# Experts' weighted rows added by index into four sums in DRAM, in place of six gathered rows per token

## The chip, the core and the metric

The kernel runs on one core of a Trainium2 chip. The metric is the device time of one execution in microseconds (us). All numbers of the profile are from one execution, taken by the hardware profiler. Engines are PE (TensorE), DVE (VectorE), ACT (ScalarE), POOL (GpSimd) and SP (SyncE, which only issues transfers here).

## What is computed

Four sequences of 512 tokens of 256 numbers, 2048 tokens in all, go through six residual blocks:

```python
x = x + 0.5 * _L0_ffn_ref(_layernorm(x), ...)   # 64 experts, the best 6 per token, and a shared one
x = x + _L0_attn_ref(_layernorm(x), ...)        # gated linear attention, 8 heads
x = x + 0.5 * _L0_ffn_ref(_layernorm(x), ...)   # the same experts again
x = x + 0.5 * _L1_ffn_ref(_layernorm(x), ...)   # 8 experts, all computed, gated
x = x + _L1_attn_ref(_layernorm(x), ...)        # softmax attention over a latent, 16 heads
x = x + 0.5 * _L1_ffn_ref(_layernorm(x), ...)
```

The change concerns the first and third line, which we call the expert layer:

```python
scores = softmax(x @ gate_weight.T)              # 64 experts in 8 groups, 3 groups kept
topk_w, topk_i = top_k(masked scores, 6)
pos = place of this token among those of its expert, in order of tokens
slot = expert * 96 + min(pos, 95)                # 96 slots per expert
buf = zeros(64 * 96, 256).at[slot].set(x[tok])   # so slot 95 keeps the last token sent there
out = (silu(buf @ Wg.T) * (buf @ Wu.T)) @ Wd.T   # per expert, 96 rows
y = sum over k of out[slot[k]] * topk_w[k]       # six rows per token
return y + shared(x)
```

There are 12288 choices for 6144 slots, so most experts overflow. All tokens past place 94 of an expert share its slot 95, and each adds the output of that one slot by its own weight.

## The kernel before

The stream x stays in SBUF as 16 tiles of 128 tokens (`k.X`). Each engine has its own instruction list in the order in which the code emits it, and waits on semaphores; nothing is reordered at run time. The program is a row of blocks, and at the end of each all engines meet.

**Routing** (`route`, once per expert layer, tile pairs m = 0 to 7). ACT normalises, SP stores the normalised rows to `xn_rows` in DRAM, PE computes the logits, DVE finds the best six experts, PE counts the places with triangular matrices, and DVE and POOL make one-hot rows from which PE builds `k.table` (96 slots by 64 experts, the token in each slot). For each token and choice DVE also writes the weight (L987) and the slot number (L904, L908). The shared expert runs in between: `gate_up`, `down` in two halves per quarter of the tokens (L697), and DVE's addition to x (L914). SP also loads the weights of the first 12 experts. The last half of `down` and its addition stand behind the table.

**Experts** (`routed_experts`, steps s = 0 to 66). In step s PE transposes the gathered rows of expert s (L1148), multiplies those of expert s-1 by gate and up (L1157), transposes the hidden rows of expert s-2 and multiplies those of s-3 by the down weights (L1174). ACT evicts the result to `sb_e_y` (L1201) and stores it to `slot_rows` in DRAM (L1203); there are two such buffers. POOL gathers 96 rows of 1 KB for each expert (L1131) into four buffers, each free again once PE has transposed it. SP loads 544 KB of weights for expert e when expert e-12 is done with its buffers.

**Combination**. In the next block POOL gathers, for each tile of 128 tokens, six sets of 128 rows from `slot_rows` (L1236), and DVE adds each by its weight to x (L1250). For the first expert layer this is in `linear_attention`, for the second in `dense_experts`. There POOL runs up to two tiles ahead, and DVE's six additions per tile are spread between the operations of a tile three places earlier. In `linear_attention` the tiles 0 to 3 come ahead of everything else; while POOL gathers them, PE folds weights of the later attention together (`fold`, L1512 and L1518) in the two score banks.

Of the kernel before, what the change touches and what calls it, by code (L numbers as in the profile page):

```python
# [5 lines left out]
ALU = mybir.AluOpType  # L6
# [20 lines left out]
AHEAD = 12  # L27
MS = 352
# [40 lines left out]
class Kit:  # L69


    def __init__(self, nc, ctx):
        self.nc, self.ctx, self.sems = nc, ctx, {}
# [4 lines left out]
    def sem(self, name):  # L78
        if name not in self.sems:
            self.sems[name] = self.ctx.enter_context(self.nc.semaphore(name))  # L80
        return self.sems[name]

# [24 lines left out]
def load_and_prepare(nc, k, w):  # L107
# [3 lines left out]
    with ExitStack() as ctx:  # L111
# [3 lines left out]
        def _(sp):  # L115
            for q in range(NT // 4):
                sp.dma_start(k.X[:, 4 * q:4 * q + 4, :], w["x"].rearrange("(q n p) d -> q p n d", p=P, n=4)[q])\
                  .then_inc(k.sem(f"x_loaded{q}"), 16)
# [7 lines left out]
        def _(pool):  # L126
# [9 lines left out]
            s.mark(pool.memset(k.chunk_keep[:, :], 1.0))  # L136
# [13 lines left out]

            s.mark(pool.memset(k.chunk_keep[:, :].rearrange("p (c s) -> p c s", s=SUB)[:, :, 0:1], 0.0))
# [40 lines left out]
def dense_experts(nc, k, r, store=None, combine=None):  # L192
# [17 lines left out]
    with ExitStack() as ctx:  # L210
# [22 lines left out]
        if combine is not None:  # L233
            rows = [[sb(f"c{combine}_rows{u}_{j}", [P, D]) for j in range(TOPK)] for u in range(2)]
# [4 lines left out]
        ps_e = [ps(f"d{r}_ps_e{j}", [P, 2, D]) for j in range(NP)]  # L239
        block = ctx.enter_context(nc.Block())  # L240
# [14 lines left out]
        def _(pe):  # L255
# [47 lines left out]

            transposed(0, 0)
            logits(0, 0)
            pe.wait_ge(we_low, (r + 1) * DC)
            tiles(pe, tile)

        @block.scalar
        def _(act):  # L310
# [33 lines left out]
            act.preload_act_table_set("natural_log_exp_and_others")  # L344
            act.wait_ge(k.sem("we1_loaded"), 16 * DC)
# [9 lines left out]
        if combine is not None:  # L355
            @block.gpsimd
            def _(pool):
                for n in range(NT):
                    gather_tile(pool, k, combine, n, n % 2, rows)

        @block.vector
        def _(dve):
# [9 lines left out]
            def statistics(n, u):  # L372
# [3 lines left out]
                if combine is not None:  # L376
                    rows_all_added(dve, k, combine, n)
# [7 lines left out]
            def add(n, u, *which):  # L385

                if combine is not None and live(n):
                    for j in which:
                        add_row(dve, k, combine, n, u, rows, j)
# [71 lines left out]
            def tile(n, u):  # L461
# [5 lines left out]
                add(n + 3, 1 - u, 0)  # L467
# [4 lines left out]
                add(n + 3, 1 - u, 1)  # L472
                weigh_odd(n, u, 1)
                add(n + 3, 1 - u, 2)
# [3 lines left out]
                add(n + 3, 1 - u, 3)  # L478

                def last_even():  # L480
                    weigh_even(n, u, 3)
                    add(n + 3, 1 - u, 4)

                def add_up():
# [3 lines left out]
                    add(n + 3, 1 - u, 5)  # L488
# [12 lines left out]

            for n in range(2):
                add(n, n, *range(TOPK))
# [8 lines left out]
            add(2, 0, *range(TOPK))  # L512
# [13 lines left out]
def route(nc, k, r):  # L526
# [7 lines left out]
    XB = 4  # L534
# [1955 lines left out]
```

## Time and profile before

| | us |
|---|---|
| median of 3 runs (lowest, highest) | 1840.82 (1838.76, 1846.98) |
| the profiled execution | 1830.69 |
| its span, first to last instruction | 1829.0 |
| PE, DVE, ACT, POOL busy | 1545.8, 1081.9, 766.6, 684.5 |
| mean granted TensorE clock | 0.932 of full |

The stages by the profile: routing 0 to 132 us, experts 132 to 303, linear attention 303 to 682, routing 682 to 804, experts 804 to 971, dense experts 971 to 1181, latent attention 1181 to 1695, dense experts 1695 to 1829. A share of busy time is a mean over stages that have different limits, so the stages are read one by one.

### The profile page before, as it was taken

The page shows a single profiled execution, that of the slowest core. Times are in us where ns is not written, and L with a number is a line of the kernel's source. Part 1 is how long each engine was busy: PE and PEld are TensorE (multiplying, and loading weights), DVE is VectorE, ACT ScalarE, POOL GpSimd, SP SyncE. Part 2 cuts the span into 40 slices and gives each one's busy share as a digit, 9 for nine tenths or more (in the row PEclk, how much of TensorE's full clock was granted, in tenths as well). Part 3 has the DMA queues.
Part 4 walks back from the last instruction along what each step waited for, and adds up shares of the span by engine and source line. Part 5 has one row for each costly group of instructions (what it writes and reads, how often), then busy time and mean ns, then how long its engine had stood idle before and what let it go on. Part 6 is the DMA issues. An engine that isn't in the chain of part 4 may idle for free. (4 is left out here: it accounts for less than half of the span.)

```text
span 1829.0 us, 26202 instructions
## 1 busy us (share of the span) xinstructions
PE 1545.8 (85%) x7678; PEld 1015.6 (56%) x7678; DVE 1081.9 (59%) x2737; ACT 766.6 (42%) x1822; POOL 684.5 (37%) x675
## 2 busy tenths in 40 slices
PE   6869995658888978869993778699999999998798
PEld 3546663425555544546662656455666666665576
DVE  6842222576775547822224888477766766663788
ACT  5523332356455435533332111266655556553211
POOL 3543333753200004633335553065545555553000
PEclk9989998679999988989996898799999999999899
DMA  8309995321100015129972221000000000000000
GB/s 245 91 12 255 296 298 177 106 65 48 35 1 1 1 44 149 48 84 285 299 230 84 77 77 52 1 0 1 1 1 1 1 1 1 1 1 1 9 17 21
DMA packets 83395, 142.55 MB, mean 78 GB/s; under 512 B 15816, under 2 KB 43312, under 8 KB 83296
## 3 DMA queue, kind: packets, MB, share of 16 engines
q1 hardware_dynamic: 53600, 90.96, 17.0%
q0 software_dynamic: 15360, 37.77, 6.9%
q10 hardware_dynamic: 14336, 12.59, 2.4%
q8 instruction: 52, 0.85, 0.2%
q14 instruction: 47, 0.39, 0.1%
HBM read 122.39 MB, written 18.87 MB: 77 GB/s over the span
## 5 line engine op out<-in xcount | busy, mean ns | idle before, releaser
L2239 POOL TENSOR_TENSOR sb_m_prob<-sb_m_prob,sb_m_rinv 128x512 f32<-128x512 f32 x256 | 258.6, 1040 | 286.1 <-DVE sb_m_rinv L2288 286.1
L2195 ACT ACTIVATE sb_m_prob<-m_ps_s,sb_m_nmax 128x512 f32<-128x512 f32 x256 | 173.6, 683 | 205.4 <-DVE sb_m_nmax L2292 205.4
L2292 DVE TENSOR_REDUCE sb_m_nmax<-m_ps_s 128x2 f32<-128x1024 f32 x128 | 156.3, 1222 | 128.0 <-PE m_ps_s L2090 127.9
L1236 POOL DMA_INDIRECT sb_c_rows<-slot_rows,sb_slot x192 | 191.4, 997 | 107.1 <-issue 51.6
L1131 POOL DMA_INDIRECT sb_e_x<-xn_rows,sb_table x128 | 117.7, 919 | 223.9 <-PE e_ps_x L1148 184.1
L1219 DVE TENSOR_TENSOR sb_e_h<-sb_e_sg,e_ps_gu 96x176 f32<-96x176 f32 x128 | 42.7, 333 | 259.7 <-ACT sb_e_sg L1195 259.7
L1157 PE MATMUL e_ps_gu<-e_wgu,sb_e_xT 128*96 128x352 f32 x512 | 180.1, 475 | 12.1 <-ACT sb_e_xT L1189 11.4
L2098 PE MATMUL m_ps_p<-sb_ident,sb_m_prob 128*128 128x128 f32 x1024 | 136.8, 274 | 15.8 <-ACT sb_m_pT L2203 11.3
L2098 PEld LDWEIGHTS m_ps_p<-sb_ident,sb_m_prob 128*128 128x128 f32 x1024 | 118.4, 141 | 41.2 <-POOL sb_m_prob L2239 14.4
L1174 PE MATMUL e_ps_y<-e_wdn,sb_e_hT 96*96 96x256 f32 x512 | 131.4, 380 | 0.0
L2089 PE MATMUL m_ps_s<-sb_m_latT_high,sb_m_qa 128*128 128x512 f32 x256 | 126.0, 492 | 1.8 <-ACT sb_m_prob L2195 1.8
L2109 PE MATMUL m_ps_v<-sb_m_pT,sb_m_lat 128*64 128x512 f32 x512 | 123.7, 605 | 0.9 <-DVE sb_m_oT L2303 0.9
L1250 DVE SCALAR_TENSOR_TENSOR sb_x<-sb_c_rows,sb_weight,sb_x 128x256 f32<-128x256 f32 (+1 forms) x192 | 92.8, 483 | 41.8 <-DMA sb_c_rows<-slot_rows,sb_slot 38.5
L686 PE MATMUL s_ps<-sb_r_xnT,sb_sguT 128*128 128x512 f32 (+1 forms) x192 | 101.1, 676 | 6.5 <-ACT sb_s_up L782 6.5
L281 PE MATMUL d_ps_e<-sb_d_we_high,sb_d_xT_high 128*128 128x512 f32 x256 | 98.6, 468 | 7.5 <-DVE sb_d_xT_low L402 7.5
L1157 PEld LDWEIGHTS e_ps_gu<-e_wgu,sb_e_xT 128*96 128x96 f32 x512 | 75.5, 167 | 52.6 <-issue 10.0
L2090 PE MATMUL m_ps_s<-sb_m_latT_low,sb_m_qa 128*128 128x512 f32 x256 | 102.1, 399 | 0.0
L1201 ACT ACTIVATE sb_e_y<-e_ps_y 96x256 f32<-96x256 f32 x128 | 48.6, 379 | 118.4 <-DMA slot_rows<-sb_e_y 90.2
L1189 ACT ACTIVATE sb_e_xT<-e_ps_x 128x192 f32<-128x192 f32 x128 | 42.3, 330 | 117.2 <-PE e_ps_x L1148 46.1
L2299 DVE COPY sb_m_pT<-m_ps_p 128x512 f32<-128x512 f32 x128 | 86.5, 676 | 3.8 <-PE m_ps_p L2098 3.8
L1746 POOL TENSOR_TENSOR sb_g_gw<-sb_g_g,sb_g_sig 128x512 f32<-128x512 f32 x8 | 10.9, 1363 | 206.0 <-ACT sb_g_sig L1658 206.0
L1434 PE MATMUL g_bank<-sb_g_xT,sb_wq 128*128 128x512 f32 x128 | 66.7, 649 | 24.9 <-ACT sb_g_zm L1619 24.8
(274 smaller groups left out, 3231.3 us busy)
## 6 DMA issues: line engine op xcount, KB each, us to landing
e_wgu<-wgu SPq DMA_DIRECT2D x128, 352.0 KB, 4.8
e_wdn<-wdn SPq DMA_DIRECT2D x128, 192.0 KB, 4.5
slot_rows<-sb_e_y ACTq DMA_DIRECT2D x128, 96.0 KB, 4.3
xn_rows<-sb_r_xn SPq DMA_DIRECT2D x16, 256.0 KB, 2.2
sb_c_rows<-slot_rows,sb_slot POOLq DMA_INDIRECT x192, 2.8
sb_x<-x SPq DMA_DIRECT2D x4, 512.0 KB, 5.3
sb_e_x<-xn_rows,sb_table POOLq DMA_INDIRECT x128, 5.0
sb_g_zm<-wqT SPq DMA_DIRECT2D x1, 2048.0 KB, 8.9
```

The source lines that it names most:

```text
L686: ins = pe.matmul(ps_s[which][0:rows, :], k.sguT[:, d, which * MS + m0:which * MS + m0 + rows], xnT[:, d, q * QT:(q + 1) * QT], start=(d = ...
L1131: pool.indirect_dma_start(x[u][:, :], None, k.xn_rows[:, :], bass.IndirectOffsetOnAxis(ap=k.table[:, e:e + 1], axis=0)).then_inc(got[u], 16)
L1157: ins = pe.matmul(ps_gu[v][:, :], xT[v][:, c, :], wgu[(u - 1) % U][:, c, :], start=(c == 0), stop=(c == DC - 1))
L1174: ins = pe.matmul(ps_y[v][:, :], hT[v][:, c, :], wdn[(u - 3) % U][:, c, :], start=(c == 0), stop=(c == 1))
L1236: pool.indirect_dma_start(rows[u][j][:, :], None, k.slot_rows[:, :], bass.IndirectOffsetOnAxis(ap=k.slot[:, n, j:j + 1], axis=0))\
L2089: pe.matmul(to[:, hh, :], q[:, hh, cols], latT[b % 2][0][:, :], start=True, stop=False)
L2090: ins = pe.matmul(to[:, hh, :], q[:, hh, cols], latT[b % 2][1][:, :], start=False, stop=True)
L2098: ins = pe.transpose(ps_p[hh][:, t, :], prob[s % 4][:, hh, t * P:(t + 1) * P], k.ident[:, :])
L2109: ins = pe.matmul(ps_v[rows_of(hh), :], lat[pair // PAIRS % 2][:, t, :], pT[pair % 2][hh][:, t, :], start=(t == 0), stop=(t == TB - 1))
L2195: act.activation(prob[s % 4][:, hh, :], ps_s[s % 2][:, hh, :], ACT.Exp, bias=nmax[s % 2][:, hh:hh + 1], accum_out=rsum[s % 2][:, hh:hh + 1 ...
L2239: pool.tensor_tensor(part, part, rinv[s % 2][:, hh:hh + 1].to_broadcast([P, T]), ALU.mult)\
L2292: dve.tensor_reduce(nmax[s % 2][:, :], ps_s[s % 2][:, :, :], AX, ALU.max, negate=True).then_inc(nmax_ready, 1)
```

## The change

1. **Routing.** Instead of six weights and slot numbers per token, DVE makes a dense row of 64 weights, splits it by place (`late`: place 95 or later) into `share`, which SP stores behind the normalised row in `xn_rows` (now rows of 320 numbers), and `over`, which stays in SBUF. The table's empty slots get the number of a row past the last token. ACT's queue writes zeros over four sums in DRAM. The last quarter's `down` is moved behind the table, and POOL issues the first four gathers inside the routing block.
2. **Experts.** ACT's eviction scales each row by its weight, which came with the gathered row. POOL adds rows 0 to 94 by index into one of four sums in DRAM (an indirect transfer that accumulates; expert e uses sum e modulo 4), and ACT's queue stores row 95 to `last_out` in SBUF. A gather for expert e+6 is issued behind the addition of expert e, into one of six buffers. There are four `sb_e_y` buffers.
3. **Combination.** SP loads the four sums in order, 128 rows each per tile. DVE adds the four up with one reduction whose input is read at a step of 256 numbers, and adds the total to x. What the shared last slots give is computed ahead of it by PE (`LastSlots`: four groups of four transposes and four products, ACT's copies, DVE's additions).
4. **Linear attention.** Four banks instead of three for projections and one instead of two for scores; the folds move to the slot u = -2.

The core of the diff:

```diff
@@ route, sync
+            def store_share(m):
+                sp.wait_ge(share_ready, g0 + m + 1)
+                sp.dma_start(shares[m], share[m % 2][:, :, :]).then_inc(share_stored[m % 2], 16)
@@ route, tensor
-                    if q:
+                    if q and q < NQ:
                         down(q - 1, 0)
+            counted()
             tabled(NPR - 1)
...
+            pe.wait_ge(unfilled_ready, r + 1)
+            pe.matmul(kept_table, k.ident[0:CAP, 0:CAP], unfilled[:, :], start=False, stop=False)
...
+            pe.wait_ge(gu_copied, 3 * (q0 + NQ))
+            down(NQ - 1, 0)
             down(NQ - 1, 1)
@@ route, scalar
             exps(0)
+            for a in range(SUMS):
+                act.dma_start(k.sums[a][0:N, :].rearrange("(p j) d -> p (j d)", j=NT).rearrange("p (q f) -> p q f", f=512),
+                              k.zeros[:, :].unsqueeze(1).to_broadcast([P, NT * D // 512, 512])).then_inc(zeroed, 16)
...
@@ route, gpsimd
+            last_hidden()
...
+            pool.wait_ge(table_ready, r + 1)
+            for e in range(XB):
+                gather_expert(pool, k, e, k.gathered[e], e)
@@ route, vector
-            def slots_capped(m):
...
-            def slots(m, capped):
...
+            def weights_of(m):
+                for i in range(2):
+                    done = s.mark(dve.scalar_tensor_tensor(out=dense[m % 2][:, i, :], in0=masked[:, i, :],
+                                                           scalar=rsum[:, i:i + 1], in1=member[m % 2][:, i, :],
+                                                           op0=ALU.mult, op1=ALU.mult))
...
+                return s.mark(dve.tensor_scalar(late[:, :, :], ps_p[:, :, :], float(CAP - 1), None, ALU.is_ge))
...
+                dve.scalar_tensor_tensor(out=share[m % 2][:, :, :], in0=dense[m % 2][:, :, :], scalar=0.5, in1=late[:, :, :],
+                                         op0=ALU.mult, op1=ALU.max).then_inc(share_ready, 1)
+                return s.mark(dve.scalar_tensor_tensor(out=k.over[:, pair_of(m), :], in0=dense[m % 2][:, :, :], scalar=0.5,
+                                                       in1=late[:, :, :], op0=ALU.mult, op1=ALU.mult))
@@ routed_experts
-    U, GA, LAG = AHEAD, 4, 3
+    U, GA, LAG = AHEAD, 6, 3
...
-                    pool.wait_ge(xT_raw, g - (GA - 1))
...
+            for e in range(XB, GA):
+                gather_expert(pool, k, e, x[e], e)
+            for e in range(E0):
+                b, earlier = e % SUMS, e // SUMS + r * (E0 // SUMS)
+                pool.wait_ge(y_ready, e + 1 + r * E0)
+                if earlier:
+                    pool.wait_ge(y_added[b], 16 * earlier)
                 pool.sem_inc(k.sem("passed"), 1)
+                pool.indirect_dma_start(k.sums[b][:, :], bass.IndirectOffsetOnAxis(ap=k.table[0:CAP - 1, e:e + 1], axis=0),
+                                        y[b][0:CAP - 1, :], None, compute_op=ALU.add).then_inc(y_added[b], 16)
+                if e + GA < E0:
+                    gather_expert(pool, k, e + GA, x[e % GA], e % GA)
...
-                        act.wait_ge(y_stored[v], (g - (3 + v)) * 8)
-                    act.activation(y[v][:, :], ps_y[v][:, :], ACT.Copy).then_inc(y_ready, 1)
+                    if earlier:
+                        act.wait_ge(y_added[b], 16 * earlier)
+                        act.wait_ge(y_last[b], 16 * earlier)
+                    act.activation(y[b][:, :], ps_y[v][:, :], ACT.Copy, scale=x[e % GA][:, D + e:D + e + 1]).then_inc(y_ready, 1)
                     act.wait_ge(y_ready, g - 2)
-                    act.dma_start(k.slot_rows.rearrange("(e c) d -> e c d", c=CAP)[s - 3], y[v][:, :])\
-                       .then_inc(y_stored[v], 16)
+                    act.dma_start(k.last_out[e:e + 1, :], y[b][CAP - 1:CAP, :]).then_inc(y_last[b], 16)
@@ combination
+def load_sums(sp, k, n, rows, a):
+    for i in range(SUMS):
+        sp.dma_start(rows[a][:, i, :], k.sums[i][n * P:(n + 1) * P, :]).then_inc(k.sem(f"rows_loaded{a}"), 16)
...
+    dve.tensor_reduce(total[:, :], rows[a][:, :, :].rearrange("p i d -> p d i"), AX, ALU.add).then_inc(k.sem("c_rows_summed"), 1)
...
+    dve.tensor_tensor(x, total[:, :], x, ALU.add).then_inc(k.sem("c_rows_added"), 1)
...
+class LastSlots:
+    def all_products(self, pe):
+        self.turn(pe, 0)
+        self.turn(pe, 1)
+        for q in range(NT // 4):
+            self.multiply(pe, q)
+            if q + 2 < NT // 4:
+                self.turn(pe, q + 2)
@@ linear_attention
-    A = 3
+    A = 4
...
-        ps_at = [ps(f"g_ps_at{u}", [P, HG, SUB]) for u in range(2)]
+        ps_at = ps("g_ps_at", [P, HG, SUB])
...
+                if u == -2:
+                    pe.wait_ge(raw_loaded, 48)
+                    pe.wait_ge(shared.out_used, 2 * (NT // 4))
+                    for n in range(FOLDS):
+                        fold(n)
```

POOL's list in the experts block, before (`e_x` are the gathered rows; the two branches are the end of one block and the start of the next):

```order
L853 TENSOR_TENSOR sb_s_gate<-sb_s_gate,sb_s_up 128x1024
L548 UNCONDITIONAL_BRANCH
L1120 UNCONDITIONAL_BRANCH
L1131 DMA sb_e_x<-xn_rows,sb_table 96x256 x64
```

and now, with what each waits for (four of the six buffers are called `e_xn`, `sums` are the sums in DRAM):

```order
L1351 DMA e_xn<-xn_rows,sb_table 96x320 x3
L584 UNCONDITIONAL_BRANCH
L1237 UNCONDITIONAL_BRANCH [waits barrier_Pool_Activation_PE_DVE_SP_gather]
L1351 DMA sb_e_x<-xn_rows,sb_table 96x320 x2
L1247 DMA sums<-sb_e_y,sb_table 2176x256 [waits e_y_ready]
L1351 DMA e_xn<-xn_rows,sb_table 96x320
L1247 DMA sums<-sb_e_y,sb_table 2176x256 [waits e_y_ready]
```

The gathers were a list of their own that waited for PE's transposes; each now stands behind an addition that waits for ACT's eviction.

PE's list at the end of routing, before (`s_ps_d` is the shared expert's `down`, `r_ps_t` the table):

```order
L675 MATMUL r_ps_t<-sb_r_hot_tok,sb_r_hot_pos 96x64 x12
L697 MATMUL s_ps_d<-sb_sdT,sb_s_gate 128x256 x6
L675 MATMUL r_ps_t<-sb_r_hot_tok,sb_r_hot_pos 96x64 x12
L729 MATMUL r_ps_x<-sb_ident,sb_r_last 64x128
L731 MATMUL r_ps_t<-sb_ident,sb_last_slot 96x64
L697 MATMUL s_ps_d<-sb_sdT,sb_s_gate 128x256 x6
```

and now:

```order
L735 MATMUL r_ps_t<-sb_r_hot_tok,sb_r_hot_pos 96x64 x12
L743 MATMUL r_ps_r<-sb_r_member_sum,sb_ones_bf 128x64
L744 MATMUL r_ps_r<-sb_r_member,sb_ones_bf 128x64
L745 MATMUL r_ps_r<-sb_r_member,sb_ones_bf 128x64
L735 MATMUL r_ps_t<-sb_r_hot_tok,sb_r_hot_pos 96x64 x12
L799 MATMUL r_ps_x<-sb_ident,sb_r_last 64x128
L801 MATMUL r_ps_t<-sb_r_unfilled,sb_ident 96x64
L803 MATMUL r_ps_t<-sb_ident,sb_last_slot 96x64
L766 MATMUL s_ps_d<-sb_sdT,sb_s_gate 128x256 x6
L766 MATMUL s_ps<-sb_sdT,sb_s_gate 128x256 x6
```

Both last halves of `down` stand behind the table, and the second has a bank of its own.

## Rows read from the trace of the kernel before

**Rows 1.** Busy PE, PEld, DVE, ACT, POOL, 200 to 240; then clock, DMA share, GB/s.

```profile
200.00:240.00 40.00, 39.13 (x193) 25.68 (x192) 9.34 (x32) 14.57 (x48) 14.70 (x16) 1.00 1.04 301
```

**Rows 2.** Transposes of gathered rows in both experts blocks: last numbers, first and last start.

```profile
L1148 PE MATMUL e_ps_x<-sb_ident,sb_e_x x128: 244/246/423, 131.9 to 293.6; 96*128 96x96 f32 x128
...
L1148 PE MATMUL e_ps_x<-sb_ident,sb_e_x x128: 244/246/423, 804.1 to 961.2; 96*128 96x96 f32 x128
```

**Rows 3.** Who waited for whom in 132 to 303: us, times, longest.

```profile
POOL sb_e_x L1131 <- PE e_ps_x L1148: 94.5, 57, 5.4
ACT sb_e_y L1201 <- DMA slot_rows<-sb_e_y: 50.1, 45, 3.3
```

**Rows 4.** Timeline (start, length) of late steps of the second experts block.

```profile
958.56 0.36 PEld L1148 LDWEIGHTS e_ps_x<-sb_ident,sb_e_x 96*128 96x128 f32 x2
...
960.94 0.36 PEld L1148 LDWEIGHTS e_ps_x<-sb_ident,sb_e_x 96*128 96x128 f32 x2
...
963.74 0.38 ACT L1201 ACTIVATE sb_e_y<-e_ps_y 96x256 f32<-96x256 f32 x1 [0.72 <-PE e_ps_y L1174]
```

**Rows 5.** Median us to landing in 128:136, 200:240, 270:290; last, a queue's total.

```profile
sb_e_x<-xn_rows,sb_table POOLq DMA_INDIRECT x6, 2.6
...
sb_e_x<-xn_rows,sb_table POOLq DMA_INDIRECT x16, 5.1
...
slot_rows<-sb_e_y ACTq DMA_DIRECT2D x9, 96.0 KB, 1.7
...
q0 software_dynamic: 15360, 37.77, 6.9%
```

**Rows 6.** Timeline at the end of the first routing block.

```profile
110.97 2.42 DVE L921 TENSOR_TENSOR sb_s_gate<-sb_s_gate,sb_s_up 96x512 f32<-96x512 f32 x1 [0.30 <-ACT sb_s_gate L788]
...
117.24 4.45 PE L697 MATMUL s_ps_d<-sb_sdT,sb_s_gate 128*128 128x256 f32 x12 [7.02 <-DVE sb_x L914]
...
123.30 0.22 DVE L1044 CAST sb_table<-r_ps_t 96x64 uint32<-96x64 f32 x1 [0.47 <-PE r_ps_t L731]
...
127.07 0.69 DVE L914 SCALAR_TENSOR_TENSOR sb_x<-s_ps_d,sb_x 128x512 f32<-128x512 f32 x1 [2.96 <-PE s_ps_d L697]
...
131.72 0.92 POOL L1131 DMA_INDIRECT sb_e_x<-xn_rows,sb_table  x1 [0.30 <-issue]
```

**Rows 7.** Groups of DVE instructions: three of routing, one of the block at 971.

```profile
L1005 DVE TENSOR_REDUCE sb_r_member<-sb_r_hot 128x128 bf16<-128x768 f32 x8 | 11.8, 1479 | 0.3
...
L900 DVE TENSOR_REDUCE sb_r_posf<-sb_r_picked 128x12 f32<-128x768 f32 x8 | 7.5, 933 | 0.0
...
L976 DVE TENSOR_TENSOR sb_r_masked<-sb_r_ex,r_ps_own 128x128 f32<-128x128 f32 x8 | 2.2, 277 | 0.1
...
L1250 DVE SCALAR_TENSOR_TENSOR sb_x<-sb_c_rows,sb_weight,sb_x 128x256 f32 (+1 forms) x96 | 46.0, 479 | 14.4 <-DMA sb_c_rows<-slot_rows,sb_slot 13.8
```

**Rows 8.** SP's issues (start, length) in routing and in linear attention.

```profile
25.75 0.47 SPq L610 DMA_DIRECT2D e_wgu<-wgu  x1
...
305.54 6.15 SPq L1339 DMA_DIRECT2D sb_g_qp<-wo  x1
```

**Rows 9.** Timeline at the head of linear attention; the last row is its first slot.

```profile
321.40 13.88 PE L1512 MATMUL g_ps_at<-sb_g_kp,sb_g_zm 128*128 128x64 f32 x64 [21.13 <-DMA sb_g_qp<-wo]
...
335.22 5.51 PE L1518 MATMUL g_ps_at<-sb_g_qp,sb_g_kp 128*64 128x256 f32 x32
...
341.61 0.30 ACT L1597 ACTIVATE sb_g_ln_var<-sb_g_mv,sb_eps 128x4 f32<-128x4 f32 x1 [0.24 <-DVE sb_g_mv L1781]
...
378.48 3.78 PE L1434 MATMUL g_bank<-sb_g_xT,sb_wq 128*128 128x512 f32 x4 [22.29 <-ACT sb_g_zm L1619]
```

**Rows 10.** Four transposes at 9 us, and the expert products of both dense blocks.

```profile
9.47 1.11 PE L637 MATMUL r_ps_x<-sb_ident,sb_r_xn 128*128 128x128 f32 x4 [2.77 <-ACT sb_r_xn L756]
...
L281 PEld LDWEIGHTS d_ps_e<-sb_d_we_high,sb_d_xT_high x128: 186/190/338, 998.4 to 1153.2; 128*128 128x128 f32 x128
...
L281 PEld LDWEIGHTS d_ps_e<-sb_d_we_high,sb_d_xT_high x128: 187/190/337, 1706.2 to 1823.2; 128*128 128x128 f32 x128
```

More of the change, by code:

```diff
@@ L239, in dense_experts @@
         ps_e = [ps(f"d{r}_ps_e{j}", [P, 2, D]) for j in range(NP)]
+        if combine is not None:
+            flat = [bank.rearrange("p a d -> p (a d)") for bank in ps_e]
+            shared = LastSlots(k, combine, flat[0:2], flat[2:4], wT)
         block = ctx.enter_context(nc.Block())
@@ L302, in tile @@
                 pair(n, u, 3)
+            if combine is not None:
+                shared.all_products(pe)
             transposed(0, 0)
@@ L306, in _ @@
             pe.wait_ge(we_low, (r + 1) * DC)
+            if combine is not None:
+                pe.wait_ge(shared.out_used, 2 * (combine + 1) * (NT // 4))
             tiles(pe, tile)
@@ L500, in tile @@
                 dve.tensor_tensor(x, ps_b[:, :], x, ALU.add).then_inc(out_ready, 1)
+            if combine is not None:
+                shared.all_added(dve)
             for n in range(2):
-                add(n, n, *range(TOPK))
+                sum_rows(n, n)
+                add_rows(n)
                 statistics(n, n)
@@ L551, in route @@
         nmr = sb(f"r{r}_nmr", [P, NT])
-        xn = [sb(f"r{r}_xn{u}", [P, 2, D]) for u in range(XB)]
+        xn = k.xn
         xnT = sb(f"r{r}_xnT", [P, DC, N])
@@ L562, in route @@
         masked = sb(f"r{r}_masked", [P, 2, E0])
+        rsum = sb(f"r{r}_rsum", [P, 2])
+        dense = [sb(f"r{r}_dense{u}", [P, 2, E0]) for u in range(2)]
+        late = sb(f"r{r}_late", [P, 2, E0])
+        share = [sb(f"r{r}_share{u}", [P, 2, E0]) for u in range(2)]
+        unfilled = sb(f"r{r}_unfilled", [CAP, E0])
         top = sb(f"r{r}_top", [P, 2, 8])
@@ L1309, in linear_attention @@
         gw = [sb(f"g_gw{u}", [P, T]) for u in range(2)]
-        rows = [[sb(f"c0_rows{u}_{j}", [P, D]) for j in range(TOPK)] for u in range(2)]
+        rows = [sb(f"c0_rows{a}", [P, SUMS, D]) for a in range(ROWS)]
+        total = sb("c0_total", [P, D])
         raw = sb("g_raw", [P, 2, 6])
@@ L1577, in _ @@
             pe.wait_ge(w_high, 2)
-            pe.wait_ge(raw_loaded, 48)
-            for n in range(FOLDS):
-                fold(n)
+            shared.all_products(pe)
             transposes(0)
@@ L1707, in slot @@
                     lns(u + 2)
+                if u == -2:
+                    for n in range(FOLDS):
+                        fold_copy(n)
                 if qs:
@@ L1729, in _ @@
             act.activation(k.wo0[:, :, :], k.wo0[:, :, :], ACT.Copy, scale=k.gnorm[:, 0:1]).then_inc(w_high, 1)
-            for n in range(FOLDS):
-                fold_copy(n)
+            shared.all_copies(act)
             deviations(0)
```

343 lines of the change are left out of this document (220 added, 123 removed).

## Prediction, written before the changed kernel ran

> **What bounds the kernel now.** I read the busy time by stretches first, then the first and last start of a few groups, then who waited for whom, and the timeline where a stage turns. In an experts block PE is busy nearly all the time and the DMA engines are saturated [rows 1]: 39.1 of 40 us, at 301 GB/s. The transposes of the gathered rows start once per expert, so their first and last start give the pace [rows 2]: 161.7 us for 63 intervals (2.57 each) and 157.1 (2.49). POOL, which gathers, is far ahead: it waits 94.5 us for PE to free a buffer. ACT waits 50.1 us, 45 times, for a store to land, because there are only two buffers [rows 3]; PE stays busy meanwhile, so those waits are near the limit and not far over it. Late in the block, where no weights are loaded any more (the last 12 steps), a step takes 960.94 - 958.56 = 2.38 us [rows 4]: PE's own pace. In the dense block at 971 it is not PE that sets the pace: its weight loads span 154.8 us there, and only 117.0 in the other dense block, which has the same products and no combination [rows 10]. (154.8 - 117.0)/13 = 2.91 us per tile is six additions of 0.479 us [rows 7] = 2.87.
>
> **Experts.** The change removes the fixed distance between gather and use. The gather for expert e+6 stands behind the addition of expert e, and that waits for ACT's eviction of e, which falls in step e+3. So a ring closes every three steps:
> - from the start of step e+3 to the eviction's end: 963.74 + 0.38 - 960.94 = 3.18 us [rows 4];
> - POOL issues the addition, then the gather: the pitch of one issue is 0.92 + 0.30 = 1.22 [rows 6];
> - from the gather's issue to its landing, L, until step e+6 may start: 2.6 with the queues free, 5.1 saturated [rows 5].
>
> 3P = 3.18 + 1.22 + L, where P is the pace. L = 2.6 gives 2.33, under PE's own 2.38; L = 5.1 gives 3.17. A step now moves 544 KB of weights, 96 rows of 1.25 KB in, and 95 KB out once, or twice if an accumulation reads what it adds to: 759 to 854 KB. At P = 2.93 this is 259 to 291 GB/s, somewhat under the 301 at which L is 5.1. So I take L = 4.4, nearer the loaded row, and P = 2.93. Fifty-one intervals with weight loads and 12 without: 51 x 2.93 + 12 x 2.38 = 178.0, against 161.7 and 157.1: +16.3 and +20.9. At the end an accumulation has to land where a store did, 2.6 against 1.7 [rows 5]: +1 per layer. Sum **+39**. The four output buffers remove the 50.1 us of ACT's waits, but the ring comes in their place. The additions themselves cost POOL an issue each, covered by the 94.5 us it waited.
>
> How 95 accumulated rows cost the queues, no row shows. Lower bound: as the gather's rows, 36864 rows of 1 KB in 6.9% of 16 engines' span of 1829 us [rows 5], 0.055 us per row on its engine, 0.33 for six rows. Upper: on few engines and read and written, rival C.
>
> **Routing.** The last hidden product, 2.42 us of DVE ahead of the table, goes to POOL, and a half of `down`, 4.45, is put behind it: the table, at 123.30, comes about 6.5 earlier. Both halves of `down` then follow each other, 8.9 us, and the last addition (127.07 + 0.69) comes 2.9 earlier [rows 6]. The first gathers are issued at the table and land under `down`, so the 2.5 us between barrier and first transpose that were their landing [rows 2, 5] are gone: -5.4 per layer, **-11**. POOL's issue beside the hidden product hides behind the same 8.9 us; without that cover it would be 3.7 late. DVE per pair: five new instructions, three of 128x128 at 0.28 [rows 7] and two half as wide (0.14 to 0.28), minus three of 12 numbers (0.14, half of it, my choice): +0.7 to 1.0, taken 0.7; DVE waits for PE about half the time here, so half of 16 x 0.7 stays: +6. Thirteen zero writes on ACT's queue at 0.47 each = +6; upper bound, if each of the eight large ones blocks as the load of `wo` did, 6.15 [rows 8], 49. I take 0.47, as most issues have it. Routing together **+1** (-11 + 6 + 6).
>
> **Linear attention.** The shared slots come first, from about 306 (the block's first load stands at 305.54 [rows 8]): four groups, each four transposes of 1.11 [rows 10] and four products of 512 columns, two thirds of the 4.45 us that twelve of 256 took [rows 6] = 2.97 at the low clock; 16.4, and 0.7 for the last addition. Then four tiles, each a reduction, an addition (0.48) and about 0.9 of statistics and gaps. The reduction reads its input at a step, as L1005 does: 1.479/768 per number gives 1.97 us for 1024; as L900, which reads in order, 1.24 [rows 7]. I take 1.97. Tiles ready at 306 + 17.1 + 4 x 3.35 = 336.5, before 341.6 [rows 9]: -5. SP's sums are 512 KB per tile and come under the shared slots. The folds, 13.88 + 5.51 = 19.4 us, fit in the 22.29 us for which PE waited at 378.48 [rows 9]: +1 for the handover; uncovered they would cost 19.4. The fourth bank loosens evictions a little: -4, a guess between 0 and -10. Together **-8**.
>
> **Dense block at 971.** If DVE sets the pace, a tile falls from 2.87 to 1.97 + 0.48 = 2.45: 13 x 0.42 = -6 (with the reduction at 1.24, -15). Its head: 971 + 17.1 + two tiles 6.7 + normalise 0.8 + halves 4.5 + 0.6 = 1000.7, where the first product stood at 998.4 [rows 10]: +2. **-4**.
>
> **Sum.** 39 + 1 - 8 - 4 = +28. The profiled execution took 1830.69, 10 below the median of the three runs, which I take as spread of the runs and not of the work: 1859 on the profile's basis, 1869 on the median's. I say **1870**.
>
> **Rivals.**
> A: as above, L near 4.4.
> B, the other side: the DMA engines have gaps once POOL no longer gathers ahead, and the ring stays near PE's pace. With the other terms at -11, the break-even is 102P + 57.2 + 2 - 318.8 = 11, so P = 2.66 and L = 3.6: below that the kernel is faster. At L = 2.8, P = 2.4, the experts give -15 and the sum is -26: 1815. With the reduction at 1.24 it is -35: 1805. For it: demand at 2.6 us per step is 292 to 328 GB/s only in the loaded 51 steps, and what can't be served at once may fall on the weights, which have 12 steps of room, rather than on the gathers. Against it: in every loaded stretch of before the gathers took 5.1.
> C: 95 rows are spread over fewer DMA engines than 96, since 95 = 5 x 19. Nineteen rows on one engine are 19 x 0.055 = 1.04 us, double or triple if read, added and written, and the gather stands behind them in the same queue: L = 5.1 + 1.5 = 6.6, P = 3.67. 51 x 3.67 + 28.6 = 215.8, twice, less 318.8, +2, -11: +104, 1945. No row of before has 95 rows in a transfer, so the trace bears it neither out nor rules it out.
> (The Trainium skill, "DMA: Bandwidth & Descriptors", section "Why a DMA increments its semaphore by 16 and not by 1", says that a transfer uses the largest number of engines up to 16 that divides the slowest dimensions, which is 5 for 95, with an exception for some direct copies from POOL's queue. By that rule C holds; the 96 rows of before would use 16. It would make the chance of C larger than I give; I hold it down since its price, not its being, needs a saturated queue.)
> D: the zero writes block ACT: of the 49 above, the 6 are in the sum and DVE's work hides part of the rest; +25 over A, 1895.
> E: the gains and the ring cancel, within 0.5%, which is about what a measurement of this kernel can tell from no change.
> That the kernel doesn't do what it says: the zeros, the additions and the reads of the sums are ordered by waits throughout, so I give it nothing.
>
> **Chances.** A 0.42, B 0.29, C 0.16, D 0.05, E 0.08. Faster by over 0.5% is B and a little of A's lower edge (0.02): 0.31; within 0.5%: 0.08; slower: 0.61. A's own range is 1850 to 1895 (L from 3.9 to 5.1). The range for 8 in 10 reaches from B's 1805 to C's 1945.
>
> **What would show it.** The pace of the transposes in the experts blocks, near 2.9 in the loaded part and 2.4 in the last 12, with PE waiting for gathered rows and POOL for `sb_e_y` (A); L by the landing of gathers in the loaded stretch, and of the additions in the same queue; if only a third of the DMA engines work on an addition, C. ACT without waits for stores. ACT's zero issues at 0.47 or longer (D). The table near 117 and the last `down` behind it; first transposes near 126.5. The reduction at 1.97 or 1.24; the head of linear attention at 336; the folds inside the gap before the first projection; the dense block's weight loads over 149 us. The prediction is wrong if the pace stays under 2.66 (faster) or goes above 3.2.

## The result: 14% slower, and the profile after

The changed kernel takes 2092.0 us (median of 4 runs, 2082.2 to 2096.0) against 1839.8 for the kernel before beside it: a ratio of 1.137, 95% interval 1.133 to 1.141. The forecast was 1870, the range 1805 to 1945. The profiled execution spans 2089.4 us where that of before spans 1829.0, so 260.4 us have to be found. Four marks cut the span into stages: the first and last transpose of gathered rows in each experts block, the first statistics of linear attention's head, and the first and last expert product of the dense blocks. The first fence is of the changed kernel, groups of PE, PEld and ACT instructions (after the duration in ns: first and last start); the transposes of one block stand in two groups, by buffer.

```profile
L1263 PE MATMUL e_ps_x<-sb_ident,e_xn x88: 244/305/423, 154.4 to 430.8; 96*128 96x96 f32 x88
...
L1263 PE MATMUL e_ps_x<-sb_ident,e_xn x88: 245/302/424, 946.1 to 1222.7; 96*128 96x96 f32 x88
...
L1782 ACT ACTIVATE sb_g_ln_var<-sb_g_mv,sb_eps x4: 281/292/298, 483.4 to 655.0; 128x4 f32<-128x4 f32 x4
...
L301 PEld LDWEIGHTS d_ps_e<-sb_d_we_high,sb_d_xT_high x128: 186/190/338, 1272.5 to 1413.7; 128*128 128x128 f32 x128
```

With the same marks before [rows 2, 9, 10]:

| stage | before | after | difference |
|---|---|---|---|
| start to first transpose | 131.9 | 154.4 | +22.5 |
| 63 steps of experts, first layer | 161.7 | 276.4 | +114.7 |
| last transpose to head of linear attention ready | 48.0 | 52.6 | +4.6 |
| from there to the first transpose of the second layer | 462.5 | 462.7 | +0.2 |
| 63 steps of experts, second layer | 157.1 | 276.6 | +119.5 |
| last transpose to first dense product | 37.2 | 49.8 | +12.6 |
| dense products with the combination | 154.8 | 141.2 | -13.6 |
| the rest | 675.8 | 675.7 | -0.1 |

Nine tenths of the loss are the two experts blocks, one tenth the routing (the row from the head of linear attention to the second layer is +0.2 only because 5 gained in that block hide 5 lost in the second routing). Who waits there, in 154 to 434 (columns as in [rows 3]), first of POOL's list and then of PE's:

```profile
POOL sums L1247 <- ACT sb_e_y L1318: 79.8, 19, 6.4
POOL sums L1247 <- issue: 12.7, 41, 0.4
...
PE e_ps_x L1263 <- DMA e_xn<-xn_rows,sb_table: 85.6, 22, 5.8
PE e_ps_x L1263 <- DMA sb_e_x<-xn_rows,sb_table: 1.6, 2, 1.0
```

Before, POOL waited for PE and PE for nothing much; now PE waits for gathered rows and POOL for evicted rows, about once in every three experts. Taken over a whole stretch the DMA engines have time left: this is the stretch of [rows 1] again, with PE at 30.3 busy in place of 39.1, the clock at 0.74, a DMA share of 0.61 and 150 GB/s in place of 301.

```profile
200.00:240.00 40.00, 30.25 (x108) 18.33 (x108) 5.41 (x18) 9.67 (x27) 21.76 (x17) 0.74 0.61 150
```

One whole round of the ring, by the timelines of PE (transposes), ACT (evictions) and POOL (start, length, what stood before):

```profile
229.43 0.58 PE L1263 MATMUL e_ps_x<-sb_ident,e_xn 96*128 96x96 f32 x2 [4.18 <-DMA e_xn<-xn_rows,sb_table]
...
234.17 0.43 PE L1263 MATMUL e_ps_x<-sb_ident,e_xn 96*128 96x96 f32 x2
...
234.42 0.47 ACT L1318 ACTIVATE sb_e_y<-e_ps_y,e_xn 96x256 f32<-96x256 f32 x1 [1.72 <-PE e_ps_y L1289]
...
235.87 1.85 POOL L1247 DMA_INDIRECT sums<-sb_e_y,sb_table  x1 [4.35 <-ACT sb_e_y L1318]
...
236.66 0.33 PE L1263 MATMUL e_ps_x<-sb_ident,e_xn 96*128 96x96 f32 x2
...
238.02 0.95 POOL L1351 DMA_INDIRECT e_xn<-xn_rows,sb_table  x1 [0.30 <-issue]
...
239.27 1.85 POOL L1247 DMA_INDIRECT sums<-sb_e_y,sb_table  x1 [0.30 <-issue]
...
243.98 0.58 PE L1263 MATMUL e_ps_x<-sb_ident,e_xn 96*128 96x96 f32 x2 [4.77 <-DMA e_xn<-xn_rows,sb_table]
```

From one late transpose to the next, 14.55 us for three experts: 5.46 to the end of the eviction (234.89), 0.98 until POOL issues the addition, 2.15 until it issues the gather, 5.96 until those rows can be transposed (the view of DMA issues has 5.4 as the median to landing in 200 to 240, 6.5 for additions). This is one of the longer rounds. Over all rounds of the first layer whose first expert stands where this one does (its number divides by three), the trace gives 13.85 on average: 4.97, 0.99, 2.15 and 5.74. The pace of the transposes is 4.52 over the first 51 intervals and 3.83 over the last 12, in the second layer 4.47 and 4.05. So the last 12 do not run at the 2.38 of [rows 4], although no weights are loaded there any more: gathers stand behind additions up to the last gather, that of expert 63.

PE runs three steps in a burst and then stands for 4 us. The three parts of this round, first step, rest of the burst, pause (busy PE, PEld, DVE, ACT, POOL; then clock, DMA share, GB/s):

```profile
229.40:234.20 4.80, 4.77 (x13) 2.85 (x14) 0.60 (x2) 0.64 (x2) 1.82 (x2) 0.50 0.52 102
234.20:239.20 5.00, 5.00 (x25) 3.11 (x23) 1.20 (x4) 2.07 (x6) 2.79 (x2) 0.98 0.57 140
239.20:243.90 4.70, 0.01 (x1) 0.00 (x0) 0.00 (x0) 0.47 (x1) 4.02 (x3) 0.71 0.95 258
```

After the pause the granted clock is 0.50, the lower level, for the whole first step (a pair of transposes takes 0.58, later in the burst 0.33), and that step needs 5.46 to its eviction. A later one takes 3.17, from 234.17 to the eviction's end at 237.34, as [rows 4] had 3.18. The third row shows what the mean of 150 GB/s hides: while PE waits for the gathered rows, the DMA engines are at 0.95 and 258 GB/s.

The routing shows the second loss on ACT's queue (the last group stands in the second layer):

```profile
14.51 16.98 ACTq L873 DMA_DIRECT2D sums<-sb_zeros  x3
31.52 7.66 ACTq L877 DMA_DIRECT2D sums<-sb_zeros  x4
39.21 0.85 ACTq L878 DMA_DIRECT2D xn_rows<-sb_zeros  x1
40.10 0.60 ACT L812 ACTIVATE sb_r_xnT<-r_ps_x 128x512 f32<-128x512 f32 x1 [25.58 <-issue]
...
821.20 10.43 ACTq L873 DMA_DIRECT2D sums<-sb_zeros  x3
```

ACT stood for 25.58 us in the first layer and 10.42 in the second while it issued the zero writes.

### The profile page after: what moved, and what is told of

Same layout as the page of the kernel before. It is cut to its first block and busy times, and to the rows that moved or that the text cites. A ratio compares the mean times of both kernels' runs of the same rounds, so it can differ in the third digit from the quotient of the medians.

```text
span 2089.4 us, 26181 instructions
## 1 busy us (share of the span) xinstructions
PE 1643.9 (79%) x7784; PEld 1063.9 (51%) x7784; DVE 1101.3 (53%) x2657; ACT 781.5 (37%) x1826; POOL 739.3 (35%) x613
## 3 DMA queue, kind: packets, MB, share of 16 engines
q0 software_dynamic: 47104, 28.41, 7.9%
## 5 line engine op out<-in xcount | busy, mean ns | idle before, releaser
L1247 POOL DMA_INDIRECT sums<-sb_e_y,sb_table x128 | 236.5, 1848 | 190.1 <-ACT sb_e_y L1318 163.2
L1272 PE MATMUL e_ps_gu<-e_wgu,sb_e_xT 128*96 128x352 f32 x512 | 221.0, 564 | 0.5 <-ACT sb_e_xT L1304 0.5
L1263 PE MATMUL e_ps_x<-sb_ident,e_xn 96*128 96x96 f32 x176 | 39.1, 316 | 176.3 <-DMA e_xn<-xn_rows,sb_table 173.4
L1289 PE MATMUL e_ps_y<-e_wdn,sb_e_hT 96*96 96x256 f32 x512 | 147.8, 417 | 0.0
L1263 PEld LDWEIGHTS e_ps_x<-sb_ident,e_xn 96*128 96x128 f32 x176 | 25.2, 172 | 203.3 <-DMA e_xn<-xn_rows,sb_table 148.7
L1272 PEld LDWEIGHTS e_ps_gu<-e_wgu,sb_e_xT 128*96 128x96 f32 x512 | 91.1, 201 | 49.3 <-issue 24.8
L1351 POOL DMA_INDIRECT e_xn<-xn_rows,sb_table x88 | 83.5, 949 | 37.3 <-issue 29.7
L1289 PEld LDWEIGHTS e_ps_y<-e_wdn,sb_e_hT 96*96 96x96 f32 x512 | 83.8, 186 | 17.7
```

What stands on the lines that cost most here:

```text
L1247: pool.indirect_dma_start(k.sums[b][:, :], bass.IndirectOffsetOnAxis(ap=k.table[0:CAP - 1, e:e + 1], axis=0), y[b][0:CAP - 1, :], None, co ...
L1272: ins = pe.matmul(ps_gu[v][:, :], xT[v][:, c, :], wgu[(u - 1) % U][:, c, :], start=(c == 0), stop=(c == DC - 1))
L1289: ins = pe.matmul(ps_y[v][:, :], hT[v][:, c, :], wdn[(u - 3) % U][:, c, :], start=(c == 0), stop=(c == 1))
```

## Experiments

Theory (ring): in the experts blocks the round through eviction, addition, gather and landing decides, so more distance between gather and use ends it, down to what POOL can issue. Rivals: the 95 rows of an addition (rival C of the prediction), the adding itself, or the transfers as such. The kernel before took 1874 in the group of e1, e2, e3 and e5, 1864 in that of c_again, e7, e8 and e9, 1840 in that of e10, e11 and e13, and 1839 beside e14, so each ratio is to the kernel before beside it. Blocks are compared by their 63 intervals from first to last transpose; across groups such a comparison carries that difference with it.

### e1_far: twelve buffers

```diff
-    U, GA, LAG = AHEAD, 6, 3
+    U, GA, LAG = AHEAD, 12, 3
```

> Twelve gather buffers instead of six, so the gather of expert e+12 stands behind the addition of e; nothing else. In the changed kernel a round of three experts takes 14.5 us: 1.0 from the eviction to the addition's issue, 2.15 for that issue, 5.96 until the gather has landed, 5.46 until the next eviction. Theory ring: with nine steps of distance in place of three that round is worth 14.5/9 = 1.6 per expert and no longer decides; what is left is POOL's own pitch, 1.85 + 0.30 + 0.95 + 0.30 = 3.40 per expert. 63 x 3.40 = 214 against 276, in both blocks: about 125 less, 1965. Rival queues (the transfers themselves are the limit, whatever the order): the pace stays at 4.4, 2090.

Measured: 1948.9, ratio 1.042 (1.033 to 1.051). The blocks: 201.7 and 202.1 in place of 276. POOL now issues without a stop (timeline of POOL):

```profile
228.82 1.85 POOL L1247 DMA_INDIRECT sums<-sb_e_y,sb_table  x1 [0.30 <-issue]
230.98 0.95 POOL L1351 DMA_INDIRECT sb_e_x<-xn_rows,sb_table  x1 [0.31 <-issue]
232.23 1.85 POOL L1247 DMA_INDIRECT sums<-sb_e_y,sb_table  x1 [0.30 <-issue]
```

The pitch is 232.23 - 228.82 = 3.41. From its first addition to its last POOL issues 52 additions with a gather behind them and 11 without: 52 x 3.41 + 11 x 2.15 = 201.0, and the trace has 203.0 and 200.6. (The expectation had 63 steps at 3.40, with a gather behind each.) A gather is now issued some 15 us ahead of its use in place of 6. The ring was the limit, and POOL's issues are the next one. Transfers as such are refuted: the same bytes were moved 75 us faster per block.

### e2_rows96, e3_plain, e13_rows90: what an addition costs

```diff
@@ e2_rows96
-  IndirectOffsetOnAxis(ap=k.table[0:CAP - 1, e:e + 1], axis=0), y[b][0:CAP - 1, :], None, compute_op=ALU.add)
+  IndirectOffsetOnAxis(ap=k.table[:, e:e + 1], axis=0), y[b][:, :], None, compute_op=ALU.add)
@@ e3_plain
-  y[b][0:CAP - 1, :], None, compute_op=ALU.add)
+  y[b][0:CAP - 1, :], None)
@@ e13_rows90
+  IndirectOffsetOnAxis(ap=k.table[0:90, e:e + 1], axis=0), y[b][0:90, :], None, compute_op=ALU.add)
```

> The addition takes 96 rows in place of 95 (row 95 is then added to its token's sum too, one contribution too many). Rival C, few engines because 95 = 5 x 19: the addition's issue falls from 1.85 towards the gather's 0.95 and its landing from 6.3 to 3 or less, the gather behind it lands at 3 to 4; round (1.0 + 1.25 + 3.5 + 4.0)/3 = 3.2 per expert, 63 x 3.2 = 202 against 276: 1940. Rival accumulation (what costs is that it reads and adds): issue and landing stay, 2090.

> The 95 rows are written by index without adding (the sums are then the last expert's rows). Rival accumulation: issue falls to 0.95 and landing to about 3, 1940. Rival C (95 rows on few engines): issue and landing stay near 1.85 and 6, time near 2090, at most 60 less for the read that is gone.

> The changed kernel with the additions cut to 90 rows (the last five of each expert are not added). Issue of the addition: 95 rows took 1.85 us and 320 packets, 96 rows 1.44 us and 102. If what counts is that 16 divides the number, 90 = 15 x 6 should look like 95: 1.8 us and over 250 packets. If it is only the number of engines that divide it (5 for 95, 15 for 90), 90 looks like 96: 1.4 us, about 100 packets, experts blocks about 237 us and not 276.

What these kernels compute is not the result: with 96 rows the last one is added once too often, plain writes keep only the last expert's rows, and with 90 five rows of each expert are left out.

Measured: 96 rows 2020.5, ratio 1.080 (1.069 to 1.091), blocks 236.7 and 240.0; plain writes of 95 rows 2019.3, 1.079 (1.069 to 1.090), blocks 237.0 and 251.0; 90 rows 2013.5 in one run, blocks 241.6 and 232.1. The first two came out between the values that their expectations set against each other (1940 and 2090). The lines of each page that tell them apart (of the core: all packets, and those under 512 bytes; of the queue: packets, MB, share; of the group: busy, mean ns, then idle time), in the order changed kernel, 96 rows, plain 95, 90 rows:

```profile
DMA packets 136729, 156.09 MB, mean 75 GB/s; under 512 B 50200, under 2 KB 94592, under 8 KB 136624
...
q0 software_dynamic: 47104, 28.41, 7.9%
...
L1247 POOL DMA_INDIRECT sums<-sb_e_y,sb_table x128 | 236.5, 1848 | 190.1 <-ACT sb_e_y L1318 163.2
```

```profile
DMA packets 110105, 156.01 MB, mean 77 GB/s; under 512 B 23448, under 2 KB 67968, under 8 KB 110000
...
q0 software_dynamic: 20480, 28.33, 7.9%
...
L1247 POOL DMA_INDIRECT sums<-sb_e_y,sb_table x128 | 184.2, 1439 | 165.2 <-ACT sb_e_y L1318 134.4
```

```profile
DMA packets 108057, 155.99 MB, mean 77 GB/s; under 512 B 30488, under 2 KB 62720, under 8 KB 107952
...
q0 software_dynamic: 18432, 28.30, 5.0%
...
L1247 POOL DMA_INDIRECT sums<-sb_e_y,sb_table x128 | 145.8, 1139 | 213.1 <-ACT sb_e_y L1318 183.1
```

```profile
DMA packets 110105, 155.23 MB, mean 77 GB/s; under 512 B 24216, under 2 KB 67968, under 8 KB 110000
...
q0 software_dynamic: 20480, 27.55, 7.6%
...
L1247 POOL DMA_INDIRECT sums<-sb_e_y,sb_table x128 | 192.1, 1501 | 153.0 <-ACT sb_e_y L1318 123.6
```

A gather had 48 packets before (15360 for 320 [rows 5]). Less 128 of these, an addition of 95 rows has (47104 - 6144)/128 = 320 packets, one of 96 or of 90 rows 112, a plain write of 95 rows 96. The issue of 1.85 us is neither the count of rows (90 take 1.50, 96 take 1.44) nor the adding alone: it is adding with 95 = 5 x 19 rows. It costs 0.41 us of issue, and the change from 95 to 96 rows takes about 38 us off a block. What 90 and 96 share and 95 doesn't is a divisor near 16, 15 and 16 against 5.

The packed trace holds the size of each packet of the queue, and the sizes show how the rows are shared out. An addition of 95 rows is 95 packets of 1024 bytes, 209 of 8 and 16 of 4, which is 16 lots of 20: five lots with 19 rows each, eleven with 19 packets of 8 bytes in their place (11 x 19 = 209), and one packet of 4 in every lot. One of 96 rows is 96 of 1024 and 16 of 4, 16 lots with six rows. One of 90 is 90 of 1024, six of 8 and 16 of 4, 15 lots with six rows and one with none (112 packets, not the 102 of the expectation; 128 x 209 = 26752 and 128 x 6 = 768 are what the pages above have under 512 bytes more than that of 96 rows). A plain write of 95 rows is five lots too, 19 rows each in packets of four rows or three. This agrees with the rule of the Trainium skill that the prediction cited ("DMA: Bandwidth & Descriptors", "Why a DMA increments its semaphore by 16 and not by 1"), and for these indirect transfers its exception does not show. The trace doesn't name the engine of a packet; that a lot is an engine is read from there being 16.

The time goes with it. From an addition's issue to the end of its last row's packet the median is 5.64 us with 95 rows and 4.11 with 96; for the gather behind it 4.58 and 3.77. With plain writes the issue is the shortest (1.14), and yet the blocks gained no more than with 96 rows: these writes sit on five lots as well, and the gather behind them needs 4.04. That the second block was 11 slower still than with 96 rows stays unexplained.

The ring stays all the same: with 96 rows PE's late transposes are 12.44 us apart (229.51 and 241.95 in that trace), 4.79 to the eviction's end, 0.84, 1.74 and 5.07. The rows behind an addition are in use 5.07 after their gather's issue there, at 196 GB/s in 200 to 280; at 301 GB/s a gather landed after 5.1 [rows 1, 5].

### e5_far96: both

```diff
-    U, GA, LAG = AHEAD, 6, 3
+    U, GA, LAG = AHEAD, 12, 3
@@ and the edit of e2_rows96
```

> Twelve buffers and 96 rows together (one contribution too many, as with 96 rows alone). If 96 rows take the issue to 0.95, POOL's pitch is 2 x 1.25 = 2.5 per expert and PE's own 2.4 to 2.57 sets the block: 63 x 2.6 = 164, the kernel about 2089 - 225 = 1865. If the issue stays at 1.85 the pitch stays 3.40 and the time is that of twelve buffers alone, 1965.

Measured: 1922.8, ratio 1.028 (1.019 to 1.036), blocks 190.5 and 191.6. The issue went to 1.44 and not to 0.95, so the pitch is 1.44 + 0.93 + 0.60 = 2.97. By it POOL would need 52 x 2.97 + 11 x 1.74 = 174 from its first addition to its last. It took 189.5 and 188.5, with 12.4 us of waiting for evicted rows in the first block.

### c_again and e7_zeros_sp: the zero writes

```diff
@@ route, scalar
-            for a in range(SUMS):
-                act.dma_start(k.sums[a][0:N, :]...
@@ route, sync (r == 1: ahead of all; r == 0: behind store(3))
+                for a in range(SUMS):
+                    sp.dma_start(k.sums[a][0:N, :]...
```

> The changed kernel once more, with nothing edited, so that the others of this group are compared with it on one chip. The group before it ran on a chip on which the kernel before took 1874 and not 1840; the ratio to it should be 1.137 again, blocks of 276 us from first to last transpose.

> The eight large zero writes are issued by SP's queue instead of ACT's (in the first routing block behind the fourth store of rows, in the second ahead of all). Theory: they cost because ACT cannot go on while its queue is full, 25.6 us at 14 us and 10.4 at 821, and not because of the bytes: about 30 less, with the first transposes at 132 to 135 and not 154. Rival bytes: SP's stores and loads behind them come as late and the block gains less than 10.

Measured: the changed kernel again 2087.8, ratio 1.121 (1.117 to 1.125) and not 1.137, since the kernel before took 24 more here and the changed one 4 less; blocks 271.7 and 279.8. With the eight large zero writes on SP (the five small ones stay with ACT and take 2.6) 2058.7, ratio 1.105 (1.099 to 1.110), 29 less. The first transpose came at 130.5, not 154.5, and the second routing, from the last projection to the first transpose, took 167.8 in place of 178.1. The same 8 MB per layer cost nothing measurable on a queue that nobody waits for (SP's own issue of the four took 10.8 us at 27.5).

### e9_one_sum and e10_three_banks: the other blocks

```diff
@@ e9_one_sum, dense_experts
-  dve.tensor_reduce(total[:, :], rows[u][:, :, :].rearrange("p i d -> p d i"), AX, ALU.add)
+  dve.tensor_copy(total[:, :], rows[u][:, 0, :])
@@ e10_three_banks, linear_attention
-    A = 4
+    A = 3
```

> In the dense block that follows the second experts block DVE copies only the first sum (128x256) where it reduced four; the other sums are loaded and not used. Theory, DVE sets the pace there: 1.87 - 0.33 = 1.5 us less per tile, 13 x 1.5 = 20, the products' span 141 to 121, near the 117 of the other dense block. Rival, the loads of the sums or what they do to the transfers set it: it stays at 141.

> The changed kernel with three banks for projections in linear attention in place of four. By the prediction the fourth bank is worth 4 us (0 to 10): from the head of the block to its last projection 289 and not 285. Rival, it is worth nothing and the 5 us gained there come from something else: 285.

Measured: with one sum copied (and the other three left out of the result) 2067.0, ratio 1.110 (1.104 to 1.115), 20.8 less than the changed kernel beside it. The products' span falls to 118.7; the copy takes 0.28 where the reduction took 1.95, and 13 x 1.66 = 21.6 of the 22.5 gained are that. DVE sets this block's pace.

```profile
L301 PEld LDWEIGHTS d_ps_e<-sb_d_we_high,sb_d_xT_high x128: 187/190/338, 1269.2 to 1387.9; 128*128 128x128 f32 x128
```

With three banks (2095.2 in one run), linear attention takes 289.6 from its head (483.5) to its last projection (773.1). With four it takes 768.0 - 483.4 = 284.6, and the kernel before took 289.6 as well (341.6 to 631.2). The fourth bank is worth those 5 us; the folds that moved and the second score bank that went cost nothing together.

### e8_best, e11_woven, e14_halves: a version that keeps the idea

e8 has twelve buffers and the zeros on SP, and adds 96 rows by a table of its own, in which row 95 points past the last token:

```diff
+            dve.tensor_scalar(k.table_add[:, :], kept_table, k.dump[0:CAP, 0:1], 0.0, ALU.max, ALU.add)
...
+  IndirectOffsetOnAxis(ap=k.table_add[:, e:e + 1], axis=0), y[b][:, :], None, compute_op=ALU.add)
```

e11 adds to it that DVE sums the first tiles between its additions of the shared slots:

```diff
-    def all_added(self, dve):
+    def all_added(self, dve, tile, tiles):
         for q in range(NT // 4):
             self.add(dve, q)
+            if q < tiles:
+                dve.wait_ge(self.out_used, 2 * (self.q0 + 1))
+                tile(q)
```

e14 adds to that two additions in order in place of the reduction with a step:

```diff
-  dve.tensor_reduce(total, rows.rearrange("p i d -> p d i"), AX, ALU.add)
+  dve.tensor_tensor(rows[:, 0:2, :], rows[:, 0:2, :], rows[:, 2:4, :], ALU.add)
+  dve.tensor_tensor(total, rows[:, 0, :], rows[:, 1, :], ALU.add)
```

> A version whose result is the reference's: twelve gather buffers, 96 rows added by a table of its own whose row 95 points past the last token, and the zero writes on SP's queue. By the sum of the single runs: 202 - 11 = 191 per experts block against 276, twice -85, and -30 of the zeros: 200 less than the changed kernel, so 1.03 times the time of the kernel before; still slower, since POOL's 1.44 + 0.30 + 0.93 + 0.30 = 2.97 per expert is above the 2.53 of the kernel before (51 x 0.44, twice = 45). Rival: with the zeros beside the weight loads the first experts start late and half of their gain is lost, 1.04 to 1.05.

> The version with twelve buffers, 96 added rows and zeros on SP, and in it the first tiles of both combinations (four in linear attention, two in the dense block) are summed by DVE between its additions of the shared slots, where it waited 2.3 and 1.0 us each for PE, and not behind them. Three of four and one to two of two tiles of 3.0 us should vanish beside PE: 9 + 5 = 14 less than the version without it (1.0058 of the kernel before), so 0.998. Rival: PE's products of the next group wait for DVE's additions, which now come 1 us late each, and only half is gained: 1.002.

> The version with the woven first tiles, and in it the four sums are added up by two additions (128x512, then 128x256) in place of one reduction of 1.96 us that reads at a step of 256 numbers. 0.60 + 0.33 for 1.87, so 0.9 less of DVE per tile; where DVE sets the pace (13 tiles of the dense block, from the run that copied one sum: 22 us for 1.54 per tile) 12 less, products' span 141 to 129, and some 3 to 5 in linear attention's tiles: 1.0016 becomes 0.993. Rival: the second addition has to wait for the first on the same engine, 0.2 to 0.3 each, and half of it is lost: 0.997.

Measured against the kernel before: e8 1873.8, ratio 1.006 (1.004 to 1.008), well below the forecast 1.03; e11 1843.6, ratio 1.002 (0.999 to 1.004); e14 1828.5 against 1839.4, ratio 0.994 (0.991 to 0.996), 0.6% faster than the kernel before. e8 is 214 less than the changed kernel beside it, where 200 were expected; the 1.03 had been worked out from that kernel's first ratio, 1.137, which was 1.121 here. Its blocks take 180.7 and 185.0. In e11 and e14 the four blocks take 175.1 to 175.4, and POOL 174.2 to 174.4 from its first addition to its last: that is the 174 of its pitch, without a pause. The code of the experts block is the same in all three, and e5's differs from it only in the table of the addition, so POOL's issues are the whole limit in e11 and e14, and in e5 and e8 something adds 4 to 15 us to them. What it is was not tried; the kernel before is slower in those two groups too (1874 and 1864 against 1840 and 1839). In e11 the span from the last transpose to the head of linear attention is 46.4 (e8 52.2), to the first dense product 43.7 (50.2): 12 gained of 14 expected, by traces of two groups. Its ratio is the 1.002 of the rival and not the 0.998 of the theory. In e14 (two groups of DVE: busy us, mean ns of one, idle before):

```profile
L1373 DVE TENSOR_TENSOR sb_c_rows<-sb_c_rows 128x512 f32<-128x512 f32 x32 | 21.9, 683 | 3.6 <-DMA sb_c_rows<-sums 3.2 <-DVE sb_g_low L1995 0.2
...
L1375 DVE TENSOR_TENSOR sb_c_total<-sb_c_rows 128x256 f32<-128x256 f32 x32 | 13.6, 425 | 1.1
```

0.68 + 0.43 = 1.11 for 1.95, and the products' span goes from 141.2 to 129.3.

## Why the prediction was wrong

- **Experts, +39, measured +234.** The mechanism was the forecast's: the ring of three steps, with PE waiting for gathered rows and POOL for `sb_e_y`. The step that failed is its sum, 3P = 3.18 + 1.22 + L with L = 4.4; each of its terms was mis-sized (first the round shown, then the mean of such rounds in the first layer). "From the start of step e+3 to the eviction's end: 3.18" is 5.46 (4.97), since the clock is at 0.50 after PE's pause; a pause that the ring makes lengthens the ring. "POOL issues the addition, then the gather: 1.22" is 0.98 + 2.15 (0.99 + 2.15): the pitch was taken from a gather, an addition of 95 rows takes twice that, and the handover from ACT had no term. "L = 4.4", bounded above by 5.1, is 5.96 (5.74). Together 8.8 became 14.55 (13.85), and the pace 4.52 in place of 2.93, above the 3.2 that the text named as proof against it. A second step failed beside it: "12 without" weight loads at 2.38. The ring closes there too, and they took 3.83 and 4.05, which is 17 and 20 us.
- **Why L was too small** is shown in part. It was bounded by the mean load; the pause shown has 258 GB/s and a DMA share of 0.95, near the loaded row, because the weights of a burst are loaded in it. The spread of 95 rows adds 0.8 (4.58 against 3.77 to the gather's last packet). What standing behind an addition adds by itself no run separates.
- **Rival C, 1945, chance 0.16.** Its mechanism is there, five lots of 19 rows, and going to 96 rows takes 76 us off the two blocks, a third of what the experts lost; the other two thirds stay with 96 and with 90 rows. It had put the whole price, 1.5, into the landing: that is 0.8 of it, and the issue, which was not in it, 0.4.
- **Rival B (faster below L = 3.6)** fell: over the first layer the rows behind an addition were in use 3.6 to 8.3 us after their gather's issue, 6.0 on average.
- **Routing, +1, measured +22.5, and +5.4 in the second layer** (last projection to table: 164.5 before, 169.9 after). "I take 0.47, as most issues have it" failed: the three large writes behind the first took 5.66 each in the first layer and 3.48 in the second, and the four small ones behind them 1.9; the prediction had 0.47 and 6.15 as bounds and chose the wrong end. The dearer end was rival D, to which it gave 0.05 and a price of 25; e7 gives 29. Without those writes the first transpose comes at 130.5, 1.4 earlier than before, where the forecast's other terms (-5.4, and +3 per layer for DVE) gave 2.4.
- **Linear attention, -8, measured -0.4 (4.6 - 5.0).** Its inside was right: -5 against -4 for the bank, nothing for the folds. The work at its head was right too: 34.1 from the block's start to the ready tiles, where 33.4 was forecast and 38.5 was before. What failed is the seam: POOL's last additions queue up (last eviction at 437.8, last issue at 441.17), and the block begins at 449.3, 18.5 after the last transpose; before it was 9.5 (303.1). The forecast had +1 for that.
- **Dense block, -4, measured -1.0 (12.6 - 13.6).** That it comes out near is luck, two misses against each other. Seam and head cost 12.6 and not 3: the seam is 8.2 longer, and the shared slots' group took 4.7 (457.91 to 462.61 in linear attention's trace) where 4.1 was summed. The reduction took 1.95 as chosen, and the products gained 13.6, not 6. That DVE sets the pace is shown by two runs. But additions that follow each other start 0.39 apart, so six of them held DVE for 2.4 and not 2.87, and the new pair holds it for 2.2: by that only 3 were to be gained. Over the products' span DVE was busy 135.2 before and 129.5 after, 5.7 less, and idle 7.9 less, 4.9 of it in waits for PE's products (7.5 against 2.6); the clock went from 0.88 to 0.94. What made PE quicker there is not shown. POOL's gathers are gone from this block, and whether they held anything up was not tried.

## What to carry to other kernels

Work that ran ahead on a queue of its own loses its distance when it is queued behind work that waits for the end of the pipeline: count the round through both, with the latencies of a loaded queue and of an engine that has just paused, and give it more steps than the pipeline has. If a sum of latencies is the forecast, each is a place to be wrong by half, and here all erred to the same side. A mean load over a stretch that alternates between bursts and pauses is no bound for what lands in the pause. Rows of an indirect addition were cheap where 15 or 16 divides their number (90, 96) and dear at 95; one row more, sent where nobody reads it, was enough.

## What the runs showed of the hardware

- An indirect transfer that adds takes POOL 1.44 us of issue for 96 rows, 1.50 for 90, 1.85 for 95; without adding 1.14 for 95; a gather of 96 rows 0.95. Packets per addition: 112, 112 and 320; by their sizes the 95 rows sit in five of 16 lots, 19 in each, and from issue to the last row's end it takes 5.64 us where 96 rows take 4.11.
- Large writes from ACT's queue block ACT: 16.98 us for three of 2 MB at 14.5 us, 10.43 at 821. With the same writes on SP's queue the kernel takes 29 us less.
- After a pause of 4 us PE's first step of an experts burst had a granted clock of 0.50 for 4.8 us, and then 0.98: 5.46 us from its start to the eviction, 3.17 for the next.
- A DVE reduction of 128x1024 with a step of 256 numbers takes 1.95 us; two additions in order with the same result take 1.11.
